# Which engine splits the second half of each expert's weights: DVE or GpSimd

## The reference, cut

```python
def _L0_ffn_ref(hidden_states, router_gate, expert_gate_up, expert_down):
    hs = hidden_states.reshape(-1, orig_shape[-1])
    logits = hs @ router_gate.T
    probs = jax.nn.softmax(logits.astype(jnp.float32), axis=-1)
    topk_scores, topk_idx = jax.lax.top_k(probs, TOP_K)
    ...
    order = jnp.argsort(ids_f)
    token_slots = order % T
    x = hs[token_slots]
    for e in range(NUM_EXPERTS):
        m = (sorted_ids == e)[:, None]
        inter = inter + jnp.where(m, x, 0) @ expert_gate_up[e]
    ...
    out = jnp.zeros_like(hs).at[token_slots].add(out_rows * scores_sorted[:, None])
```

## Time and profile before

| | us |
|---|---|
| median of 3 runs | 1629.73 (1624.77 to 1634.55) |
| profiled execution | 1625.41 |
| its span, first to last instruction | 1623.7 |
| TensorE busy in the span | 1473.8 (91%) |
| DVE busy | 1041.0 (64%) |
| ACT busy | 765.4 (47%) |
| GpSimd busy | 648.8 (40%) |

### The profile page before, as it was taken

One profiled execution on the slowest core, in us unless ns is written; L12 is line 12 of the kernel. 1 busy time (PEld: TensorE's weight loads), 2 busy tenths in 40 slices (PEclk: granted clock), 3 DMA queues, 4 the chain that ended last, 5 costly groups with the idle time before them and its releaser, 6 DMA issues. The chain is left out here.

```text
span 1623.7 us, 32907 instructions
## 1 busy us (share of the span) xinstructions
PE 1473.8 (91%) x8665; PEld 1190.9 (73%) x8666; DVE 1041.0 (64%) x3154; ACT 765.4 (47%) x2010; POOL 648.8 (40%) x834
## 2 busy tenths in 40 slices
PE   5899999999999999968999799996963999999997
PEld 4788888888888788746777677776962777777775
DVE  4777777777777777756888788887664233332232
ACT  3777777776767677743322223221332323333322
POOL 3011111111111111015888368872764555555553
PEclk9999999999999999988999999996556999999999
DMA  5543433344334443456211341113883555555652
GB/s 160 127 115 100 102 85 100 91 104 103 99 91 104 104 104 91 120 208 229 53 52 52 129 148 53 52 33 133 180 206 70 104 102 99 98 99 98 102 101 44
DMA packets 89729, 172.24 MB, mean 106 GB/s; under 512 B 26336, under 2 KB 26336, under 8 KB 88608
## 3 DMA queue, kind: packets, MB, share of 16 engines
q1 hardware_dynamic: 59840, 115.12, 26.8%
q0 software_dynamic: 18176, 35.80, 12.4%
q10 hardware_dynamic: 11616, 20.27, 4.1%
HBM read 78.10 MB, written 44.79 MB: 76 GB/s over the span
## 5 line engine op out<-in xcount | busy, mean ns | idle before, releaser
L1149 PE MATMUL ps_y<-pairs,taps 128*128 128x288 f32 x1280 | 311.6, 406 | 7.0 <-DVE prods L1275 3.8
L1149 PEld LDWEIGHTS ps_y<-pairs,taps 128*128 128x128 f32 x1280 | 242.7, 190 | 75.4 <-issue 8.7
L860 ACT ACTIVATE probs<-neg_scores,neg_max 128x256 f32<-128x256 f32 x512 | 255.2, 505 | 26.6 <-DVE neg_max L661 26.6
L661 DVE CUSTOM_DVE_ANT_0 neg_scores<-ps_scores,alibi 128x256 f32<-128x256 f32 x512 | 194.9, 418 | 90.2 <-PE ps_scores L526 61.6
L870 ACT ACTIVATE probs_t<-ps_probs_t 128x512 f32<-128x512 f32 x208 | 124.1, 597 | 130.2 <-PE ps_probs_t L537 130.2
L1623 POOL DMA_INDIRECT out<-y_row,back x72 | 113.3, 1573 | 170.2 <-DMA out<-y_row,back 134.2
L537 PE MATMUL ps_probs_t<-ident,probs 128*128 128x128 f32 x1024 | 159.3, 280 | 9.1 <-ACT probs L860 9.1
L410 POOL COPY inv_wide<-inv_sum 128x512 f32<-128x512 f32 x32 | 20.6, 675 | 316.9 <-DVE inv_sum L677 316.9
L2026 DVE TENSOR_TENSOR st_lo<-ps_x,st_hi 128x512 fp32r<-128x512 f32 x72 | 49.8, 692 | 145.9 <-ACT st_hi L1798 145.8
L1180 ACT ACTIVATE q_ring<-q_g 128x512 f32 (+1 forms) x64 | 40.2, 630 | 215.8 <-DVE ps_y L1268 204.8
L537 PEld LDWEIGHTS ps_probs_t<-ident,probs 128*128 128x128 f32 x1024 | 124.3, 143 | 22.9 <-ACT probs L860 9.5
(11 more groups left out here) (197 smaller groups left out, 3596.7 us busy)
## 6 DMA issues: line engine op xcount, KB each, us to landing
q_stack<-q_hi SPq DMA_DIRECT2D x128, 128.0 KB, 2.3
k_stack<-k_hi SPq DMA_DIRECT2D x128, 128.0 KB, 2.3
taps<-kernel_pad SPq DMA_DIRECT2D x64, 256.0 KB, 3.1
x_in<-in_x SPq DMA_DIRECT2D x16, 512.0 KB, 3.3
q_stack<-q_lo SPq DMA_DIRECT2D x64, 128.0 KB, 2.3
k_stack<-k_lo SPq DMA_DIRECT2D x64, 128.0 KB, 2.3
x_rows<-x_mid SPq DMA_DIRECT2D x16, 512.0 KB, 2.9
ctx_g<-in_ctx_t SPq DMA_DIRECT2D x2, 4096.0 KB, 12.2
```

The source lines that it names most:

```text
L661: last = dve.tensor_tensor_reduce(neg_scores[h % 2][:, tt, :], ps_scores[h % 2][:, tt, :], alibi[h % 2][:, P - P * tt:P - P * tt + T], -Q_ ...
L860: last = act.activation(probs[h % 2][:, tt, :], neg_scores[h % 2][:, tt, :], ACT.Exp, bias=neg_max[par][:, h, tt:tt + 1], scale=-1.0, accu ...
L1149: last = pe.matmul(ps_y[par][:, lc, :].rearrange("p (b q) -> p b q", b=GB)[:, :, 0:PAIRS], taps[r][:, block_cols:block_cols + P], pairs[r] ...
```

## The change

GpSimd does the half-1 remainders. In its queue the split of expert b-1's half 1 stands behind the eight scatters of batch b, and expert 7's behind all of them. DVE keeps half 0.

```diff
-                route_steps(pool, scatter_pairs)
+                def route_step(k, par, last):
+                    scatter_pairs(k, par, last)
+                    if not (first_round(k) and par == 0):
+                        e = batch_no(*batch_before(k, par))
+                        wait_apart(pool, w_gu_hi_ready, e * 2 + 2, passed)
+                        split_lo(pool, 1, e)
+
+                route_steps(pool, route_step)
+                pool.wait_ge(w_gu_hi_ready, 2 * NE)
+                split_lo(pool, 1, NE - 1)
...
                         e = batch_no(*batch_before(k, par))
-                        for half in range(2):
-                            dve.wait_ge(w_gu_hi_ready, e * 2 + (half + 1))
-                            split_lo(dve, half, e)
+                        dve.wait_ge(w_gu_hi_ready, e * 2 + 1)
+                        split_lo(dve, 0, e)
...
-                for half in range(2):
-                    dve.wait_ge(w_gu_hi_ready, 2 * NE - 1 + half)
-                    split_lo(dve, half, NE - 1)
+                dve.wait_ge(w_gu_hi_ready, 2 * NE - 1)
+                split_lo(dve, 0, NE - 1)
```

## The result

The changed kernel takes 1644.83 us (median of five runs, 1643.67 to 1645.79) and the kernel before 1629.73 (1624.77 to 1634.55). The ratio is 1.009, 95% interval 1.0071 to 1.011: slower by about 15 us, where 1650 was forecast and slower by more than 0.5% held most of the chance. The profiled execution took 1643.67 us, 18.3 more than the one of before; that one was near the lower end of its runs.

What follows compares the result with a forecast made beforehand. GpSimd was taken to pace the routing stage. Splits +17.1, waits -0.8, long scatters -1.5 and tail +7.4 summed to +22.2 us: 1647.6 on the profiled execution, 1651.9 on the median, forecast 1650, range 1637 to 1664.

Steps and rivals of the forecast that it cites:

- GpSimd paces the stage and its splits go on the path: Routing stage: GpSimd sets its pace, so six splits ahead of the last batch's scatters add 17.1 us.
- A split: One 128x1024 subtract on GpSimd: 2.35 us, or 2.85 with its turn, between 2.5 and 3.6.
- The turn around it: GpSimd's change from scatter to split to scatter: taken as 0.5 us, between 0.30 and 1.03.
- The waits: GpSimd's waits for DVE ahead of scatters: 6.8 us go, 6.0 come, -0.8 us in all.
- the loop: SP's half-1 load waits for GpSimd's split, then ACT, TensorE and DVE's destinations follow: 18.7 us against GpSimd's 16.7.
- The holding of DVE: Rival: GpSimd's split holds DVE's small two-input operations ahead of batches 3, 5 and 7; up to +7, 1657, chance 0.08.
- GpSimd's 512-element folds: Reason given against DVE standing during splits: these GpSimd operations took an even 1266 ns on average beside a busy DVE.
- DVE operations of 2 us beside a split: Routing stage: listed among the signs that would show the forecast wrong.
- Long scatters: Scatters lengthened by 5.1 us in all under DVE's splits; one DVE split fewer per batch gives -1.5 us, between -3 and 0.
- The tail: Last scatter to first gather: split 6, load, ACT, split 7 and gather's start, 13.4 instead of 6.0 us, +7.4.
- Slow loads: Rival: stores sharing the DMA engines make half-1 loads take 10 us, three waits of 5; +9, 1659, chance 0.10.
- The scatter's 0.97 as GpSimd's own time: Routing stage: forecast took a scatter's 0.97 us as GpSimd's own time; rival of mostly queue waiting: 1614, chance 0.06.

Runs made afterwards that it cites:

- e3: Changed kernel with GpSimd only raising the semaphore in place of each split, half 1's remainder left out: 1635.95 us against 1633.96, ratio 1.0013.
- e10: Changed kernel with the split between the fourth and fifth scatter and two buffers for half 1: 1637.16 us against 1627.12, ratio 1.0059.
- e1: Changed kernel with GpSimd's subtracts replaced by fills that read nothing, half 1's remainder left out: 1647.79 us against 1633.96, ratio 1.0077.
- e6: Changed kernel with fills instead of GpSimd's subtracts and two buffers for half 1: 1637.66 us against 1629.93, ratio 1.004.
- e9: Kernel before with two buffers by turns for half 1, DVE doing both halves: 1626.88 us against 1627.12, ratio 0.9999.
- e2: Changed kernel with two buffers by turns for half 1: 1640.3 us against 1633.96, ratio 1.0032.
- e5: Changed kernel with half 1 of experts 6 and 7 given back to DVE: 1646.71 us against 1633.96, ratio 1.0063.
- e4: Changed kernel with the split between the fourth and fifth scatter, one buffer for half 1: 1640.67 us against 1629.93, ratio 1.0065.

## Why the prediction was right, and where it wasn't

- *GpSimd paces the stage and its splits go on the path.* Right. With the work gone (e3) the price goes, with every wait gone (e10) some 8 us stay.
- *A split.* 2.35 was forecast and 2.37 measured. The turn around it was mis-sized: 0.5 was taken, between 0.30 and 1.03, and it is 0.17 in place of a usual 0.30. So six splits cost 13.4, not 17.1, below the lower bound of 15.0, which allowed no turn shorter than a scatter's and didn't take off the 0.30 that stands between two scatters anyway.
- *The waits.* -0.8 was forecast and 0.0 measured, but by another sum: three waits of 2.0 from the loop, against four of 1.7 beyond the turn. The loop is there (e1 and e6: 3.3 us without held pairs, 0.5 without its buffer too). The holding of DVE, a rival with a chance of 0.08 and a price of up to 7, came true beside it, and did not add to the loop, since both delay the same scatter: a held pair ends with the split, whenever the rank came. The step that failed is the reason against that rival, that GpSimd's 512-element folds ran even beside a busy DVE; the number for it was a mean over 64, which can't show that, it looked at GpSimd's side, and the one that stood was DVE. DVE operations of 2 us beside a split, which the prediction listed as a sign against it, were there (2.60 and 2.98).
- *Long scatters.* -1.5 was forecast and +0.4 measured. The step that failed is that one split a batch instead of two would lengthen fewer scatters. A scatter that starts within a DVE split ends some 0.85 us behind the end of that one split. In batch 3 of after, the split ended at 1177.82 and the scatter, begun at 1176.77 and 1.91 us long, at 1178.68:

```profile
1176.60 1.22 DVE L1505 TENSOR_TENSOR w_gu_lo<-w_half,w_gu_hi 128x1024 fp32r<-128x1024 f32 x1 [0.33 <-DVEq L1945]
```

  So the first split of a pair does the lengthening, and taking the second away gives nothing back: seven scatters stand long beside splits in after, eight before. (Those eight lie in seven batches, two in the last; the prediction counted eight batches.) How much the scatters are lengthened depends on where the splits fall, and differs by about 2 us between two kernels that order the work of DVE and GpSimd alike (60.15 in the kernel before, 58.03 in e9).
- *The tail.* +7.4 was forecast and +3.56 measured, by the chain of steps that was forecast. Two terms were too large: the load landed in 3.5 us, not 6.0, and the gather followed the split after 0.15, not 1.0; the split's turns of 0.5 fell away too. The forecast took the load between the shortest and the median of transfers that all had company; this one had little. Loads in after, from issue to landing:

```profile
DMA to landing us min/median/max: 3.5/5.2/7.1
```

- *Slow loads.* Did not come. The halves landed within 7.1 us, where one took 14.9 before: why is not shown; the two halves are loaded apart in time now.
- *The scatter's 0.97 as GpSimd's own time.* Right: in the recorded spans splits and scatters never overlap.

So the sum of 22.2 became 17.4 in the profile, and 15 in the medians. Two terms were too dear, the splits by 3.7 and the tail by 3.8, and two too cheap, the waits by 0.8 and the scatters by 1.9; that these partly cancel is luck, and so is that the last scatter ended at 1246.14 where 1246 was forecast.

## What to carry to other kernels

Before work is moved to an idler engine, look at the stage in which it lands: an engine that is busy 40% of the span can be the one that paces that stage. Look at what the moved instruction releases as well: a buffer that it frees goes with it into the new queue, and loads, copies and whoever waits for them then run in that queue's order; a second buffer or another place in the queue takes that part back, but not the engine's own time. And a sum of waits isn't additive: two causes that delay the same instruction cost as much as the later one.

## What the hardware showed unexpectedly

*Who is held.* Beside a subtract on GpSimd, DVE instructions with two inputs from SBUF took until about its end, but so did some with one: the cast of `dest` (2.90 us instead of 0.17, e2), `ratio_sum` (2.89 instead of 0.17, e5), the normalisation `xn_c` (3.32 instead of 0.55, e4). Beside fills, which only write, the pair and the split went free (0.29 and 1.23, e1), while casts and `ratio_sum` were held (1.46 in e6, 1.74 in e1). Not held in after were `place`, with an input from PSUM (0.19), and the one-column casts of `take` beside the last split (0.15).

*From when.* The recorded start of a split on GpSimd doesn't tell who came first. DVE's split of expert 1 in after began 0.44 us ahead of GpSimd's (at 1159.26, while GpSimd's scatter was still running), and in e4 one began 0.61 us behind GpSimd's (at 1238.71, 2.36 us):

```profile
1158.82 3.90 DVE L1505 TENSOR_TENSOR w_gu_lo<-w_half,w_gu_hi 128x1024 fp32r<-128x1024 f32 x1 [0.33 <-DVEq L1945]
...
1239.32 2.84 DVE L1505 TENSOR_TENSOR w_gu_lo<-w_half,w_gu_hi 128x1024 fp32r<-128x1024 f32 x1 [1.06 <-ACT w_gu_hi L1775]
```

The first took 3.90 us instead of 1.23 and ended 1.10 us behind GpSimd's split, the second 2.84 and ended 1.09 behind; in e2, e5 and e10 splits that began 0.43 to 0.48 us ahead took 3.91, 3.91 and 3.95 and ended 1.09 to 1.10 behind. GpSimd's own split was never longer than 2.5 us. And the pair of batch 5 in e2 began at 1199.79; with its usual 0.29 it would have ended 0.43 us before the recorded start of the split (1200.51), yet it ended with the split. So the holding sets in ahead of the recorded start, and whether DVE or GpSimd was first in these cases is open.

*The other way.* DVE's splits hold GpSimd's scatters. In the twelve profiles 80 scatters start within a DVE split, from 0.07 us behind its start to 0.1 us ahead of its end (times within a merged pair are estimates), and all end 0.83 to 0.87 us behind its end, whether that makes them 0.97 or 2.00 us long.

The turn on GpSimd depends on what precedes: 0.30 us from scatter to scatter, none from scatter to subtract, 0.17 from subtract to scatter, and 0.64 from fill to scatter.
